# State space scan of a hybrid stack: the skip term u·D goes into y's PSUM sum by matmuls with diagonal matrices

## What is computed

```
x, z = split(rmsnorm(x) @ W_in)            # 512 channels each
u = silu(depthwise_causal_conv(x))
dt, B, C = split(u @ W_xp); delta = softplus(dt @ W_dt + b_dt)
h[t] = h[t-1] * exp(delta[t] * A) + delta[t] * B[t] * u[t]
y[t] = sum_n h[t, :, n] * C[t, n] + u[t] * D      # the term u * D is the skip term
out = (y * silu(z)) @ W_out
```

## Time and profile before

| | us |
|---|---|
| median of 3 runs | 1826.14 |
| lowest and highest | 1825.59, 1828.66 |
| the profiled execution, its own time | 1823.52 |
| its span in the trace | 1821.7 |

### The profile page before, as it was taken

How to read it: one execution, slowest core, us unless ns; L and a number is a source line. 1 busy time by engine, 2 the same in 40 slices (tenths; PEclk the granted TensorE clock), 3 DMA queues, 4 the chain that set the end, 5 groups by cost and what they waited for, 6 DMA issues and landing times. The chain is left out here.

```text
span 1821.7 us, 26108 instructions
## 1 busy us (share of the span) xinstructions
PE 1576.4 (87%) x8448; PEld 1221.7 (67%) x8448; DVE 1235.7 (68%) x2586; ACT 936.3 (51%) x1976; POOL 691.5 (38%) x624
## 2 busy tenths in 40 slices
PE   5989868979998988867876887888999897999889
PEld 3767658967776888334533444666888685788777
DVE  5888747757777778599968996444666534666643
ACT  5555445756665565554435543224665443666543
POOL 4999833324222222075714765102221232222232
PEclk9999989989999999989998999998999898999999
DMA  3212122111112220100010000001112111111111
GB/s 111 82 64 66 35 95 81 59 51 33 46 46 86 75 76 14 49 1 1 1 49 1 0 1 6 7 10 51 41 46 75 35 69 56 33 46 46 54 68 46
DMA packets 29708, 82.47 MB, mean 45 GB/s; under 512 B 6054, under 2 KB 10924, under 8 KB 27324
## 3 DMA queue, kind: packets, MB, share of 16 engines
q1 hardware_dynamic: 28444, 75.10, 12.6%
q0 software_dynamic: 1184, 6.37, 1.0%
HBM read 80.41 MB, written 1.05 MB: 45 GB/s over the span
## 5 line engine op out<-in xcount | busy, mean ns | idle before, releaser
L812 POOL TENSOR_TENSOR head_low<-head,head_high 128x512 fp32r<-128x512 f32 x64 | 81.8, 1279 | 474.3 <-ACT head_high L802 473.6
L2168 POOL TENSOR_TENSOR rings<-xp,Bs 128x512 f32<-128x512 f32 x128 | 193.7, 1515 | 163.1 <-DVE state L2107 82.9
L1708 POOL TENSOR_TENSOR experts_low<-experts,experts_high 128x1536 fp32r<-128x1536 f32 (+1 forms) x64 | 144.4, 2260 | 280.6 <-ACT experts_high L1654 161.1
L1161 ACT ACTIVATE probs<-banks,neg_max 128x512 f32<-128x512 f32 (+3 forms) x256 | 131.7, 527 | 150.2 <-DVE neg_max L1072 150.2
L1956 PE MATMUL banks<-rings,ident 128*128 128x512 f32 x256 | 140.3, 648 | 66.1 <-DVE rings L2136 66.1
L2107 DVE TENSOR_TENSOR_SCAN state<-banks,rings 128x512 f32<-128x512 f32 x128 | 155.4, 1215 | 0.0
L2042 ACT ACTIVATE banks<-delta,A 128x512 f32<-128x512 f32 x128 | 88.4, 692 | 119.2 <-DVE state L2107 108.3
L201 PE MATMUL banks<-experts_high,xnT_high 128*128 128x384 f32 (+1 forms) x384 | 139.9, 364 | 8.0 <-POOL experts_low L1708 8.0
L1405 DVE SCALAR_TENSOR_TENSOR hidden<-banks,weight,act_out 128x96 f32<-128x96 f32 (+1 forms) x192 | 62.7, 368 | 115.7 <-ACT act_out L1373 115.2
L201 PE MATMUL banks<-experts_low,xnT_high 128*128 128x384 f32 (+1 forms) x384 | 137.9, 359 | 0.0
L201 PE MATMUL banks<-experts_high,xnT_low 128*128 128x384 f32 (+1 forms) x384 | 137.6, 358 | 0.0
(11 more groups left out here) (284 smaller groups left out, 4752.3 us busy)
## 6 DMA issues: line engine op xcount, KB each, us to landing
head<-in_heads SPq DMA_DIRECT2D x64, 384.0 KB, 3.1
experts<-in_experts SPq DMA_DIRECT2D x16, 1152.0 KB, 5.2
experts<-in_experts SPq DMA_DIRECT2D x16, 768.0 KB, 4.3
values<-in_values SPq DMA_DIRECT2D x32, 256.0 KB, 3.2
coef<-in_spline_coef POOLq DMA_DIRECT2D x8, 768.0 KB, 4.7
idx<-in_lut_idx SPq DMA_DIRECT2D x16, 134.0 KB, 2.1
Cs<-in_w_in SPq DMA_DIRECT2D x2, 1024.0 KB, 4.9
x<-in_x SPq DMA_DIRECT2D x2, 512.0 KB, 4.5
```

Source lines behind the costliest of these rows:

```text
L1161: last = nc.scalar.activation(prob_tile(i), score_tile(i), ACT.Exp, bias=neg_max[:, i:i + 1], scale=QK_SCALE, accum_out=row_sum[:, i:i + 1])
L1708: nc.gpsimd.tensor_tensor(parts[gpar][1][:, columns], raw[gpar][:, columns], parts[gpar][0][:, columns].bitcast(FP32), ALU.subtract)\
L2168: nc.gpsimd.tensor_tensor(inflow[:, step % INFLOWS], du[:, c], Bs[:, n], ALU.mult)\
```

## The change

The skip term is no longer added by VectorE. GpSimd makes for each chunk a 128x128 matrix with D on its diagonal (four operations per sequence, ahead of its wait for the first stored rows, behind a wait for `vec`). TensorE multiplies it with u of the chunk into the same PSUM sum, right behind the matmul of state 12 (steps 24 and 25, 56 and 57). `take_y` is one operation, PSUM times silu(z). The semaphore `y_taken` is gone; TensorE waits for `gated_y` in its place before it writes a bank again, and for the four matrices before step 0.

```diff
--- before.py
+++ after.py
@@ -1765,7 +1765,7 @@
     spread, stored = m.sig("bc_spread"), m.sig("bc_stored")
     inflow_ready, decay_ready, scanned = m.sig("inflow_ready"), m.sig("decay_ready"), m.sig("scanned")
     product_ready, summed = m.sig("product_ready"), m.sig("summed")
-    y_taken, gated_y, joined = m.sig("y_taken"), m.sig("gated_y"), m.sig("joined")
+    skip_ready, gated_y, joined = m.sig("skip_ready"), m.sig("gated_y"), m.sig("joined")
     multiplied, bent, hidden_ready = m.sig("gate_up_done"), m.sig("gated"), m.sig("hidden_ready")
     dve_chain = m.sig("dve_chain")
     DECAYS, INFLOWS, PRODUCTS = 2, 4, 3
@@ -1790,6 +1790,7 @@
     NORM_TURN = {NORM + 7: 0, NORM + 12: 1}
     NORM_STORE = {NORM + 11: 0, NORM + 16: 1}
     NORM_ROOT = NORM + 4
+    SKIP = 12
     JOIN_AT = {2 * NS + 3: 0, 2 * NS + 5: 1}
 
     sb = m.local(ctx)
@@ -1802,6 +1803,7 @@
     w_out = sb("w_out", [P, KC, D])
     vec, A = sb("vec", [P, KC, 7]), sb("A", [P, KC, NS])
     select, split = sb("select", [6 * NS, 2 * NS], BF16), sb("bc_parts", [6 * NS, T], BF16)
+    skip = sb("skip", [P, KC, P])
     act_out, hidden = sb("act_out", [P, HALF]), [sb(f"hidden{i}", [P, HALF]) for i in range(2)]
 
 
@@ -1942,6 +1944,7 @@
         pe.wait_ge(dt_parts.sem, dt_parts.at(KC))
         multiply(0)
 
+        pe.wait_ge(skip_ready.sem, skip_ready.at(KC))
         pe.wait_ge(z_ready.sem, z_ready.at(KC))
         pe.wait_ge(first_stored.sem, first_stored.at(FIRST))
         pe.sem_inc(summed.sem, PRODUCTS)
@@ -1950,11 +1953,13 @@
             c, n = channel_of(step), state_of(step)
             if c >= 2 and n == 0:
 
-                pe.wait_ge(y_taken.sem, y_taken.at(c - 1))
+                pe.wait_ge(gated_y.sem, gated_y.at(c - 1))
 
             pe.wait_ge(product_ready.sem, product_ready.at(step + 1))
             nc.tensor.matmul(y_psum(c), m.ident[:], product[:, step % PRODUCTS], start=n == 0, stop=n == NS - 1)\
               .then_inc(summed.sem, 1)
+            if n == SKIP:
+                nc.tensor.matmul(y_psum(c), skip[:, c], u[:, c], start=False, stop=False)
             if step + FIRST < SPREADS:
                 if step:
 
@@ -2110,14 +2115,11 @@
         def take_y(c):
 
             dve.wait_ge(summed.sem, summed.at(2 * NS * (c // 2 + 1) - 1 + c % 2 + PRODUCTS))
-            nc.vector.scalar_tensor_tensor(u[:, c], u[:, c], vec[:, c, 6:7], y_psum(c), ALU.mult, ALU.add)\
-              .then_inc(y_taken.sem, 1)
-            dve.wait_ge(y_taken.sem, y_taken.at(c + 1))
             if c < 2:
                 dve.wait_ge(z_ready.sem, z_ready.at(c + 1))
             else:
                 dve.wait_ge(z_gated.sem, z_gated.at(c - 1))
-            nc.vector.tensor_tensor(u[:, c], u[:, c], silu_z[:, c], ALU.mult).then_inc(gated_y.sem, 1)
+            nc.vector.tensor_tensor(u[:, c], y_psum(c), silu_z[:, c], ALU.mult).then_inc(gated_y.sem, 1)
 
         scan(0)
         for step in range(STEPS):
@@ -2153,6 +2155,10 @@
     def gpsimd(pool):
 
         nc.gpsimd.tensor_tensor(m.x_of[b][:], m.x_of[b][:], m.xn[:], ALU.add).then_inc(xn_added.sem, 1)
+        pool.wait_ge(vec_loaded.sem, vec_loaded.at(16))
+        for c in range(KC):
+            nc.gpsimd.tensor_scalar(skip[:, c], m.ident[:], vec[:, c, 6:7], 1.0, ALU.mult, ALU.mult)\
+              .then_inc(skip_ready.sem, 1)
         pool.wait_ge(first_stored.sem, first_stored.at(FIRST))
         for step in range(STEPS):
             c, n = channel_of(step), state_of(step)
@@ -2177,7 +2183,7 @@
                      (softplus_step, 3), (delta_ready, KC), (first_spread, FIRST), (first_stored, FIRST),
                      (spread, SPREADS - FIRST), (stored, SPREADS - FIRST), (inflow_ready, STEPS),
                      (decay_ready, STEPS), (scanned, STEPS + DECAYS), (product_ready, STEPS),
-                     (summed, STEPS + PRODUCTS), (y_taken, KC), (gated_y, KC), (joined, KC), (multiplied, ITEMS),
+                     (summed, STEPS + PRODUCTS), (skip_ready, KC), (gated_y, KC), (joined, KC), (multiplied, ITEMS),
                      (bent, ITEMS), (hidden_ready, ITEMS)):
             s.close(n)
 
```

## The result

The changed kernel takes 1828.89 us, median of 14 runs (1827.12 to 1833.66); the kernel before, measured in turn with it, 1826.11 (1821.61 to 1830.36, 14 runs). The ratio is 1.0021, with a 95% interval of 1.0012 to 1.0030. The forecast was 1821.8 and the range 1818.8 to 1826.0: the result is 2.9 us above the range and on the other side, slower where faster was forecast. The profiled execution took 1830.91 us.

What follows compares the result with a forecast made beforehand. The prediction took VectorE to pace the scan. Per layer 1.2 + 0.2 + 0.76 = 2.16 us, 4.3 for two, taken from the median 1826.1 gave 1821.8 us, range 1818.8 to 1826.0.

Steps and rivals of the forecast that it cites:

- What bounds the kernel now: State space layers: VectorE sets the scan's pace, standing still in the first half only for ScalarE's tanh, 7.0 us.
- Part 1: Takings of y at steps 32 and 33: one operation fewer, the product inherits GpSimd's wait; gain 1.2 us per layer.
- rival C: Takings at steps 32 and 33: no lock on the product, gain 2.3 us per layer, time 1819.6; chance 0.10.
- Part 2: Takings at the layer's end: TensorE limits the gain, weights can load ahead; 0.2 us per layer, between 0 and 0.4.
- Part 3: Skip matmuls, steps 24, 25, 56 and 57: hidden in TensorE's idle time, cost 0; clock kept, 0.76 us won per layer.
- The 0.76: Wait before the gate of step 29, in us per layer, won because the skip matmuls keep TensorE's clock from falling.
- Rival B: Step 29's gate: clock falls anyway or hadn't fallen in other executions, no 0.76 to win; 1823.3 us, chance 0.33.
- Rival E: VectorE's saving is waited for at the tanh of step 37; only 0.2 us per layer stays, 1825.7; chance 0.07.
- Part 4: Ahead of the scan: GpSimd's four matrix operations, below 2.1 us, and TensorE's changed waits are hidden; cost 0.
- D: Behind step 32: TensorE at half clock through a gate's chain, 2.5 us lost, +1.1 per layer, 1828.3; chance 0.08.

Runs made afterwards that it cites:

- y_only: The changed kernel without the matrices, skip matmuls and their wait; y taken the new way, skip term left out: 1825.19 us, ratio 0.9988.
- mm_only: The kernel before with the matrices, the wait and the eight skip matmuls added beside the old taking: 1831.79 us, ratio 1.0024.
- before_pad34: The kernel before with 34 satisfied waits (17 instructions) added to TensorE's queue per state space layer: 1831.47 us, ratio 1.0023.
- before_delay18: The kernel before with eighteen small chained VectorE writes behind the second state space layer, one run: 1830.59 us.
- after_again: The changed kernel run once more without an edit: 1830.02 us, ratio 1.0009 to the kernel before.
- best: The changed kernel with VectorE's two recurrence operations exchanged, 222 satisfied TensorE waits per layer and GpSimd's two added waits: 1825.39 us, ratio 1.0001.
- after_pool_later: The changed kernel with GpSimd's inflow of steps 36 and 37 also waiting for VectorE's products of steps 32 and 33: 1831.24 us, ratio 1.0033.
- after_swap: The changed kernel with VectorE's first two recurrence-stage operations exchanged, h scaled before w_c is negated: 1822.86 us, ratio 0.9981.
- before_late_wc: The kernel before with the load of w_c issued behind that of skip in the second recurrence stage alone: 1828.59 us, ratio 1.0015.
- after_pad222: The changed kernel with 222 satisfied waits (111 instructions) added to TensorE's queue per state space layer: 1823.84 us, ratio 0.9991.
- before_pad256: The kernel before with 256 satisfied waits (128 instructions) added to TensorE's queue per state space layer: 1826.46 us, ratio 1.0002.

## Why the prediction was wrong, point by point

**What bounds the kernel now** held: VectorE paces the scan, and its waits are for the tanh.

**Part 1 was right.** Steps 33 to 36, which hold both takings, take 11.0 and 10.3 us (the two layers) instead of 12.2 and 11.5: 1.2 each. y_only shows the same 11.0 and 10.3, mm_only the old 12.2 and 11.5, so the taking alone does it. The product that inherits the wait ended 0.56 and 0.55 behind GpSimd, where 0.54 and 0.55 were taken; rival C is out. The Trainium skill, "SBUF — State Buffer", section "Who interferes with whom", has two SBUF inputs contend with GpSimd and one not, with the first to issue ahead; the trace agrees, 0.67 for the operation with one SBUF operand and 1.40 for the product behind it.

**Part 2** was 0.1 per layer, not 0.2.

**Part 3**: the matmuls delay nothing at either place, and the clock was kept. Steps 30 to 33 take 5.9 us instead of 6.8 in both layers of every kernel that has the skip matmuls. But before_pad34 shows 5.9 in both layers as well, y_only in one, and so does before_delay18, whose first layer is the kernel before's instruction for instruction; none of them has these matmuls. The 0.76 can thus be had without the cause that the prediction gave it, and whether the matmuls made it here isn't shown. Rival B was right in this, that one execution doesn't show what every execution does.

**Rival E was partly right.** The next gate, of step 37, gives some of it back. In the changed kernel it waits 0.84 where steps 33 to 36 came sooner:

```profile
869.50 0.42 DVE L2144 SCALAR_TENSOR_TENSOR act_out<-act_out,banks 128x256 f32<-128x256 f32 x1 [0.84 <-ACT act_out L2058]
```

Steps 36 to 40 take 11.9 and 12.5 us instead of 11.2 (after_again: 12.2 and 11.4), so 0.2 to 1.3 of the gain returns. The prediction's argument against E was that the chain to this gate begins with VectorE's own products and moves with them. The rows show why it didn't move. In both kernels the granted clock is 0.50 over 861 to 865, at the end of and behind TensorE's wait of 4.93 and 4.33 us for the product of step 33. Then, before and in the changed kernel:

```profile
865.00:867.00 2.00, 2.00 (x5) 0.96 (x4) 2.00 (x3) 0.69 (x1) 1.91 (x2) 0.60 0.03 8
865.00:867.00 2.00, 2.00 (x5) 1.28 (x4) 2.00 (x4) 0.98 (x2) 1.74 (x2) 0.50 0.00 0
```

VectorE's scans there come 0.9 us sooner, but the clock rises no sooner, and TensorE's gate and up of that item begin at 867.14 instead of 867.34. Of 0.9 us won the tanh gets 0.2. The first layer's opening, start to first scan, also took 49.9 instead of 47.8 in the profiled execution, but not in after_again (47.8), and y_only, best, after_pool_later and before_delay18 show it too: a matter of the execution. So the layers gained 0.2 in one execution, 3.4 in the second and 4.0 in after_swap, of 4.3 forecast.

**Part 4 is the step that failed.** It costed the matrices, the waits and, with Part 3, the skip matmuls in time alone ("Cost 0"), found no work waiting behind them, and the sum then stopped at the layers' end. GpSimd's four operations did take 0.376 each, 1.5 us of the 2.1 allowed, well ahead of the scan. But 17 more instructions per layer stand in TensorE's code, and they move every later load of it. One of them fell onto the start of R2, where it delays a 64 KB load by 1.2 us (0.7 in the second execution), with GpSimd's hold on VectorE and a lower clock behind it. From R1's start to the end the changed kernel loses 8.0 and 6.9 us in its two executions, before_pad34 5.1, before_late_wc 3.2. Less what the layers gained, 0.2 and 3.4, that makes +7.8 and +3.5 us. The medians of the two sets show +2.8 and +3.4, so the second execution is like most runs and the first is not. The chain of cause is shown in three links: added instructions alone make the loss (before_pad34), a shift by a whole piece unmakes it (after_pad222, before_pad256), and late weights alone make R2 longer (before_late_wc). The sizes are less settled. Where R1 takes 53, R2 is 49.5 without the piece (after_pad222) and 54.6 to 55.0 with it, 5 us and more. `h` accounts for 2.3 to 2.5 of it, 9.0 to 9.2 behind the start against 6.7; the remainder goes with the granted clock, which over the first 20 us of after_pad222's R2 is 0.84 where the changed kernel has 0.58 and 0.66:

```profile
1173.80:1193.80 20.00, 15.87 (x54) 7.72 (x55) 7.56 (x22) 1.92 (x5) 4.76 (x2) 0.84 0.07 14
```

Late weights alone took that clock from 0.74 to 0.66 (before_late_wc); why the fall is larger where R1 takes 53 no run separates, and the 1.3 us behind R2 weren't traced further.

**The rivals.** D, the only one that was slower, had TensorE at the lower clock while a gate's chain runs, behind step 32. Such a fall is there, but in the kernel before as well (0.50 over 861 to 865 in both), and what reached VectorE of it is the wait under E, 0.84 in the first layer and 1.5 in the second, not D's 2.5 in each. The loss lay in the two recurrence stages and behind them, where no rival looked at all. The chance of 0.04 for slower came from this.

## What to carry to other kernels

A change that adds instructions can cost something even where all its work is hidden: it moves the loads of that engine's code, in every stage behind it, and one of them may fall beside a small load that a stage waits for. It need not: 256 waits more per layer cost nothing here. Before a difference of 0.2 to 0.3% is put down to the work of an edit, run the kernel before with as many idle instructions added, and the changed one with its count filled up to a whole piece; the pair says what is placement. And when a lock between two engines is taken off one operation, look at which operation comes next: half of the gain went there.

## What the runs showed of the hardware

- TensorE's code comes during the run, 42 pieces of 16,384 bytes over this span, 0.69 MB in all. That is 0.2% of the DMA engines' time; with one piece beside it a 64 KB load still took 3.5 us instead of 2.3 (3.0 in a second execution).
- 256 satisfied waits of TensorE per layer do nothing measurable to the time (1.0002); 34 of them cost 4.5 us (1826.94 to 1831.47), where they move a piece from R1's start onto R2's.
- The two recurrence stages have the same work, and take 50.5 and 51.5 us or 52 to 53.4 and 49.2, with the granted clock of their first 20 us at 0.83 and 0.74 or at 0.62 to 0.75 and 0.91. In one execution, 0.6 us of delay was enough to pass from the one to the other.
- VectorE's operation by a scalar with one SBUF input, in place on 32x256, takes longer beside a GpSimd operation that began first, too (0.29 us, and 1.47, 1.83, 1.85 and 2.02).
